# Six banks and a second gate buffer for the first feed-forward, and a later place for norm steps and projections

## The reference

```python
x = x + L0_attn(norm(x))   # 8 heads of 64, keys and values from a latent of 64
x = x + L0_ffn(norm(x))    # silu(x w1) * (x w2); gelu(. h1); gelu(. h2); . w3   (hidden 1024)
x = x + L1_attn(norm(x))   # 16 heads of 16, rotary positions on q and k
x = x + L1_ffn(norm(x))    # silu(x w_gate) * (x w_up); . w_down   (hidden 768)
```

## Time and profile before

| | |
|---|---|
| median of 3 runs | 2740.22 us (2734.58 to 2742.14) |
| the profiled execution | 2743.78 us, span 2741.9 us |
| PE busy | 2489.0 us, 91% of the span |
| DVE busy | 1502.1 us, 55% |
| ACT busy | 1357.9 us, 50% |
| POOL busy | 998.3 us, 36% |
| mean granted TensorE clock | 0.955 of full speed |

### The profile page before, as it was taken

The page is one execution under the profiler, slowest core; times in us unless marked ns, Lnnn a source line. Parts: engine busy times, 40 slices in busy tenths (PEclk is TensorE's granted clock), DMA queues, the critical chain, the costliest instruction groups (busy, mean ns, idle before and its releaser), DMA issues.

```text
span 2741.9 us, 38992 instructions
## 1 busy us (share of the span) xinstructions
PE 2489.0 (91%) x15333; PEld 1493.5 (54%) x15333; DVE 1502.1 (55%) x1965; ACT 1357.9 (50%) x1816; POOL 998.3 (36%) x656
## 2 busy tenths in 40 slices
PE   6888888888889799999999999999999999999888
PEld 4344444444444477777777777644444444443677
DVE  6555666566656322322122122378989889897454
ACT  3344444444334344444444444257777777778533
POOL 1454555555455534564564564420000000000333
PEclk8999999999999899999999999989999999999999
DMA  2111121211111243544544544523231312221222
GB/s 69 39 55 45 64 69 47 82 51 53 57 40 40 84 139 134 191 166 139 189 165 143 184 166 142 168 85 70 46 72 31 70 48 42 69 44 23 65 76 66
DMA packets 139912, 241.81 MB, mean 88 GB/s; under 512 B 28272, under 2 KB 88688, under 8 KB 139376
## 3 DMA queue, kind: packets, MB, share of 16 engines
q1 hardware_dynamic: 139728, 239.29, 28.5%
HBM read 198.20 MB, written 52.03 MB: 91 GB/s over the span
## 4 chain that ended last, share of the span: by engine, by line
PE 53%; DVE 3%; DMA 3%; ACT 3%; issue 2%; POOL 1%; SPq 1%; DVEq 0%; ACTq 0%; POOLq 0%
PE m_R L110 37%; PE m_O L110 10%; PE m_X L110 4%; DMA m_ln_x<-x 2%; DVE m_ln_x L181 1%; DMA x<-m_xres 1%; ACT m_P L1533 1%; PE m_X L202 1%; DVE m_ln_stat L159 1%; PE m_X L1930 1%; POOL m_ln_rstd L176 1%; SPq L1435 0%; ACT m_gate L1592 0%; POOL m_act0l L1814 0%; PE m_X L1938 0%
## 5 line engine op out<-in xcount | busy, mean ns | idle before, releaser
L1669 DVE TENSOR_REDUCE m_mraw<-m_R 128x2 f32<-128x1024 f32 x512 | 625.8, 1224 | 104.1 <-PE m_R L110 99.4
L1533 ACT ACTIVATE m_P<-m_R 128x1024 f32<-128x1024 f32 x512 | 524.4, 1026 | 170.3 <-PE m_R L110 167.7
L538 ACT ACTIVATE a_P<-a_S 128x1024 f32<-128x1024 f32 x256 | 248.6, 1023 | 178.2 <-PE a_S L110 178.2
L110 PE MATMUL m_O<-m_P,m_V 128*17 128x256 f32 x4096 | 333.6, 398 | 2.8 <-ACT m_P L1533 1.1
L110 PE MATMUL a_O<-a_P,a_V 128*64 128x512 f32 x1024 | 283.3, 680 | 0.0
L661 DVE TENSOR_REDUCE a_mraw<-a_X 128x2 f32<-128x1024 f32 x168 | 205.3, 1222 | 135.3 <-PE a_X L110 135.3
L1786 POOL TENSOR_TENSOR m_act0l<-m_xf,m_act0h 128x512 fp32r<-128x512 f32 x128 | 165.1, 1292 | 297.4 <-ACT m_xf L1597 167.3
L819 POOL TENSOR_TENSOR a_accp<-a_accp,a_P 128x1024 f32<-128x1024 f32 x96 | 229.1, 2386 | 87.5 <-ACT a_P L538 77.9
L110 PE MATMUL m_R<-m_Q,m_K 64*128 64x512 f32 x1024 | 259.1, 502 | 1.8 <-DVE m_mraw L1669 1.5
L110 PE MATMUL m_R<-m_act0l,m_wt 128*128 128x512 f32 x640 | 260.5, 407 | 0.0
L110 PE MATMUL m_R<-m_act0h,m_wt 128*128 128x512 f32 x640 | 259.8, 406 | 0.1
(11 more groups left out here) (231 smaller groups left out, 4302.1 us busy)
## 6 DMA issues: line engine op xcount, KB each, us to landing
m_wt<-wcopy SPq DMA_DIRECT2D x176, 512.0 KB, 3.3
m_ln_x<-x SPq DMA_DIRECT2D x24, 512.0 KB, 3.9
m_xres<-x SPq DMA_DIRECT2D x96, 128.0 KB, 3.2
m_K<-bounce_k SPq DMA_DIRECT2D x96, 128.0 KB, 4.2
m_Q<-bounce_q SPq DMA_DIRECT2D x192, 64.0 KB, 2.7
a_tile<-in_L_ffn_tiles SPq DMA_DIRECT2D x22, 512.0 KB, 3.7
wcopy<-in_L_ffn_tiles SPq DMA_DIRECT2D x22, 512.0 KB, 4.9
x<-m_xres SPq DMA_DIRECT2D x64, 128.0 KB, 2.1
```

The lines of the kernel that those rows point to most:

```text
L110: return pe.eng.matmul(out, lhsT, rhs, start=start, stop=stop, skip_group_check=True)
L538: act.eng.activation(P[n % NP][:, :, :], psS[n % 2][:, :, :], ACT.Exp, scale=SCALE).then_inc(s_exp)
L1533: act.eng.activation(P[h % 4][:, :, :], pair(key)[:, :, :], ACT.Exp, scale=SCALE).then_inc(R.free(key))
L1669: dve.eng.tensor_reduce(mraw[u % 2][:, at, :], pair(key)[:, :, :], AX.X, ALU.max).then_inc(R.free(key))
```

## The change

Ring Y gets six banks up to slot 480 and its two old ones after that. The gate has two buffers; the second is a part of the exponent buffer `P[3]`, for which the raw `wo` weights move to another tile (`TON`). ACT takes a gate tile of a slot before the high part of the up tile of the slot before. For the second attention, statistics, scaling, turns, projections and values move from slots 12 to 32 to slots 15 to 40; the next block's norm load, statistics and scaling move ahead, to slots 25, 32 and 36. The rope load moves from slot 42 to 46. In the last part, statistics and scaling go from slots 1 and 3 to 2 and 4. POOL's `norm.power` goes to the end of its slot.

```diff
-    C_LOAD, C_STATS, C_SCALE, C_TURN = 10, 12, 13, (14, 16)
-    PROJECT = {18: ("k", 0), 22: ("q", 0), 26: ("k", 1), 30: ("q", 1)}
-    VALUES = {20: 0, 24: 1, 28: 2, 32: 3}
-    B_LOAD, B_STATS, B_SCALE, B_TURN = 34, 40, 42, (46, 50)
+    C_LOAD, C_STATS, C_SCALE, C_TURN = 10, 15, 18, (22, 24)
+    PROJECT = {26: ("k", 0), 30: ("q", 0), 34: ("k", 1), 38: ("q", 1)}
+    VALUES = {28: 0, 32: 1, 36: 2, 40: 3}
+    B_LOAD, B_STATS, B_SCALE, B_TURN = 25, 32, 36, (46, 50)
@@ norm_at
-        if s in (1, 3) and k + 1 < NB:
-            return norm_of["d", k + 1], int(s == 3)
+        if s in (2, 4) and k + 1 < NB:
+            return norm_of["d", k + 1], int(s == 4)
@@
+    def y_slots():
+        early = sum(len(ended_at(H)) for H in range(START - ML - 8))
+        return [i % 6 if i < early else 4 + i % 2 for i in range(len(y_order()))]
@@
-        Y = Ring(p, "y", 2, y_order())
+        Y = Ring(p, "y", 6, y_order(), slots=y_slots())
@@
-        xf, gate = [...], p.sb("gate", [128, 512])
+        xf, gate = [...], [p.sb("gate", [128, 512])[:, :], P[3][:, 0, :]]
@@ sync
-                if s == 42 and 1 <= k < NB:
+                if s == 46 and 1 <= k < NB:
                     load_rope(k)
@@ leave (ACT; last_silu likewise)
-                    if g:
-                        act.wait_ge(*Y.emptied(("up", *divmod(g - 1, MT))))
+                    if g >= 2:
+                        act.wait_ge(*Y.emptied(("up", *divmod(g - 2, MT))))
@@ scalar loop
+                if send_high_at(H):
+                    send_high(*send_high_at(H)[1:])
+                for key in ended_at(H):
+                    if key[0] == "gate":
+                        leave(key)
                 for key in ended_at(H - 1):
                     if key[0] == "up":
                         gate_high(key)
@@ gpsimd loop
-                if norm_at(H) and norm_at(H)[1] == 0:
-                    norm.power(pool, norm_at(H)[0])
                 ...
                 if last_pair_at(H - 1):
                     last_low(*last_pair_at(H - 1))
+                if norm_at(H) and norm_at(H)[1] == 0:
+                    norm.power(pool, norm_at(H)[0])
```

More of the change, by code:

```diff
@@ L1232, in ffn_attention_ffn @@
         banks = p.ps("R", [128, 6, 512])
-        psO, psX, psY = p.ps("O", [128, 512]), [p.ps("X", [128, 512])], [banks[:, 4 + i, :] for i in range(2)]
+        psO, psX, psY = p.ps("O", [128, 512]), [p.ps("X", [128, 512])], [banks[:, i, :] for i in range(6)]
         psR = [[banks[:, 2 * i + j, :] for j in range(2)] for i in range(3)]
         X = Ring(p, "x", 1, x_order())
-        Y = Ring(p, "y", 2, y_order())
-        R = Ring(p, "pair", 3, pair_order(), slots=pair_slots(), before={2: [Y.emptied(key) for key in y_order()[-2:]]})
+        Y = Ring(p, "y", 6, y_order(), slots=y_slots())
+        last_y = {Y.slot(key): Y.emptied(key) for key in y_order()}
+        R = Ring(p, "pair", 3, pair_order(), slots=pair_slots(), before={i: [last_y[2 * i], last_y[2 * i + 1]] for i in range(3)})
         psD = [x for bank in psR for x in bank]
@@ L1260, in ffn_attention_ffn @@
         act_buf = [[p.sb(f"act{i}{j}", [128, MT, 512], F32R) for j in "hl"] for i in range(2)]
-        xf, gate = [p.sb(f"xf{i}", [128, 512]) for i in range(2)], p.sb("gate", [128, 512])
+        xf, gate = [p.sb(f"xf{i}", [128, 512]) for i in range(2)], [p.sb("gate", [128, 512])[:, :], P[3][:, 0, :]]
         yt = [p.sb(f"yt{i}", [128, 512]) for i in range(2)]
@@ L1589, in leave @@
                     g = 8 * key[1] + key[2]
-                    if g:
-                        act.wait_ge(*Y.emptied(("up", *divmod(g - 1, MT))))
-                    act.eng.activation(gate[:, :], bank[:, :], ACT.Silu, scale=scol[:, 0, key[2]:key[2] + 1]).then_inc(Y.free(key))
+                    if g >= 2:
+                        act.wait_ge(*Y.emptied(("up", *divmod(g - 2, MT))))
+                    act.eng.activation(gate[g % 2], bank[:, :], ACT.Silu, scale=scol[:, 0, key[2]:key[2] + 1]).then_inc(Y.free(key))
                 elif key[0] == "hidden":
@@ L1605, in last_silu @@
                 act.wait_ge(*Dr.filled(key))
-                if g:
-                    act.wait_ge(*Dr.emptied(("dup", *divmod(g - 1, LT))))
-                act.eng.activation(gate[:, :], psD[Dr.slot(key)], ACT.Silu, scale=SC).then_inc(Dr.free(key))
+                if g == 1:
+                    act.wait_ge(s_pv, NT * NU)
+                elif g >= 2:
+                    act.wait_ge(*Dr.emptied(("dup", *divmod(g - 2, LT))))
+                act.eng.activation(gate[g % 2], psD[Dr.slot(key)], ACT.Silu, scale=SC).then_inc(Dr.free(key))
             def last_high(k, m):
@@ L1725, in up @@
                 dve.wait_ge(s_lo, fs(key) - 1)
[L1726 removed]
+                dve.eng.scalar_tensor_tensor(xf[fs(key) % 2][:, :], psY[Y.slot(key)][:, :], scol[:, 1, key[2]:key[2] + 1], gate[g % 2],
                                              ALU.mult, ALU.mult).then_inc(Y.free(key))
@@ L1733, in last_up @@
                 dve.wait_ge(s_dlo, g - 1)
-                dve.eng.scalar_tensor_tensor(xf[g % 2][:, :], psD[Dr.slot(key)], SC, gate[:, :], ALU.mult, ALU.mult).then_inc(Dr.free(key))
+                dve.eng.scalar_tensor_tensor(xf[g % 2][:, :], psD[Dr.slot(key)], SC, gate[g % 2], ALU.mult, ALU.mult).then_inc(Dr.free(key))
             def last_residual(x):
```

9 lines of the change are left out of this document (4 added, 5 removed).

## The result

The changed kernel took 2662.1 us (median, 2652.3 to 2667.9), a ratio of 0.972 to the kernel before (95% interval 0.9685 to 0.976). Timed again beside two experiments it gave 2665.5 us against 2741.3, ratio 0.9725 (0.9711 to 0.9738), 75.9 us less. 2670 was forecast, 70 us less. The profiled execution took 2667.9 us, span 2666.1.

The account below looks back on a forecast made before the run. PE was taken to set the time, so only its waits and slow running could be won: 37.2 + 17.5 + 5.4 + 23.5 + 4 - 12.6 - 5 = 70 us off the 2740.2 median, 2670 us; range 2652 to 2692.

Parts of the forecast that it names:

- The wait in front of the turn: Feed-forward, blocks 1 to 7: PE's 37.2 us waiting for DVE's norm scaling goes, with 17.5 us of half clock.
- The cover of 1.7 us: Feed-forward turn moved eight slots later: at least 1.7 us of PE work left over, so the wait costs nothing.
- The eighth turn: Turn k = 8, in the second attention: its 3.94 us wait and 1.5 us of clock go, 5.4 us together.
- Six banks: Feed-forward gate and up products: small waits for a bank go, 2.9 us in each of eight blocks, 23.5 us.
- The new wait: Start of the second hidden layer: PE waits 2.1 us for POOL's low part in six blocks, 12.6 us back.
- The clock behind the new wait: Feed-forward: two of six blocks pay 2.5 us of slow clock after PE's wait for POOL, 5 us.
- The last part: After the second attention: shorter waits for the scaling, by 0.2 to 0.5 us in 7 blocks, and earlier out_low; 4 us.
- the sign given: Last part: 22.5 us a block would show the forecast right.
- (a): Feed-forward: POOL later than counted, clock falls each time; six waits cost 36 us instead of 17.6, 2688; chance 0.20.
- (b): Feed-forward: POOL in time because ACT or PE is later than counted; 17.6 us less, 2652; chance 0.13.
- (c): Feed-forward gates: small gaps are handovers that more banks don't remove; 23.5 us less gain, 2693; chance 0.11.
- (d): Weights come late behind the store's landing on SP, two tiles by 5 us each per block; 2754; chance 0.03.

Follow-up runs that it names:

- the second profile: The changed kernel unaltered, profiled again when timed beside two later kernels: 2665.5 us, ratio 0.9725 to the kernel before.
- The one-gate run: The changed kernel with one gate buffer and ScalarE's old order in the feed-forward, six banks kept: ratio 0.976 to the kernel before.
- later slots alone: The kernel before with only the last part's statistics and scaling one slot later and the power at the slot's end: ratio 0.9947.
- two buffers alone: The changed kernel with all slots and the power's place put back, keeping six banks, two gate buffers and ScalarE's new order: ratio 0.9894.
- the added product: The changed kernel with one more 1.25 us product in POOL's queue ahead of the rotation of k1: 2676.9 us, ratio 0.9791.
- a kernel without the wait: The changed kernel with later power, the low part inside the rotation of k1 and one gate buffer in the last part: 2641.5 us, ratio 0.964.
- the one-buffer kernels: Kernels with one gate buffer in the last part: the changed kernel so altered, ratio 0.9723; with later power and low part inside the rotation too, 0.964.
- the kernel with the later power: The changed kernel with the next block's statistics, scaling and power four slots later: 2653.9 us, ratio 0.9685.

## Why the prediction was right

The likeliest case came about. Its terms:

- **What bounds it.** Right: what was gained in the feed-forward is, but for 1.6 us, time in which PE stood or ran at half clock.
- **The wait in front of the turn, 37.2 us, and 17.5 for the clock.** Right, both gone; the ledger's 2.5 us of clock is the size that was forecast. The cover of 1.7 us held.
- **The eighth turn, 5.4 us.** Measured 4.9, from the transposes of the first unit's maxima in the second attention to those of the fifth's (116.3 us before, 111.4 after; 108.0 in the second profile). In all kernels with the early slots the whole second attention took 778.8 to 782.2 us, in all with the later ones 769.7 to 780.7.
- **Six banks, 2.9 us a block.** 2.6 (18.43 less 15.82). The one-gate run shows that banks, and not gate buffers, bring it; the second buffer is worth 0.4 us a block, which is the last up tile's low part that the prediction called a close fit.
- **The new wait, 2.1 us each, 12.6 in all.** 1.82, 10.9 in all, with its place and cause as named. Counted from the same P, POOL's low part ended at 22.7 (22.4 before the 0.4 for the scalings) and PE stood ready at 20.9 (20.7). The 0.4 us that I added for the scalings were wrong: under 0.1 came of them. I had read them from the earlier trace rows as POOL being put back; there POOL's two products beside the scalings took 1.26 us each, not longer than alone, and the 0.15 us between them was a wait for ScalarE. Block 7 has no power and no scalings in its queue, and its wait is 0.85, 0.97 less: the power. The wait for the query's DMA did go, as counted, but whole; of its 3.96 us only 0.85 came back. With these sizes the phase adds up to 37.2 + 17.5 + 20.9 + 3.1 - 10.9 - 4.7 = 63.1; 1.6 us of the 64.7 are not accounted for.
- **The rule of "SBUF — State Buffer", section "SBUF: two separate sides" of the Trainium skill**, by which POOL could stand for 1.4 us. The trace does not agree with that size: POOL's product beside the scalings took 1.35 us and not 1.29, while VectorE's four took 4.40 and not 1.38. In this queue VectorE stood, POOL hardly. What the last section shows of who starts first does agree with the rule.
- **The clock behind the new wait, 5 us.** 3 x 1.6 = 4.7 in one profile, 6 x 1.6 = 9.4 in the other. The size of one was too large and the number of blocks too small; how many there are changes from one execution to the next.
- **The last part, 4 us: the term that was mis-sized.** It brought 7.8 us (4.5 in the second profile), and little of it where the sum had it. The step had the scaling at +14.7 and it ends at +14.1. It took the scalings as slow as before, but only one whole product of POOL's, not two, now falls on them (2.57 us and not 3.43). The +14.7 does not follow from its own numbers either: 11.7 + 3.43 is 15.1. And the turns shown are the late ones. Over all seven, PE waits nearly as long as before, since two of them have gone from 0.89 to 1.86 us:

```profile
PE m_R L202 <- DVE m_ln_x L181: 18.6, 7, 3.7
```

```profile
PE m_R L202 <- DVE m_ln_x L181: 18.2, 7, 3.1
```

Before first, after second: 0.4 us. The other long waits of this part, for low parts of the norm and of the attention's output (the prediction mentions the latter without a price of their own), fell from 5.3 to 1.6 us. The rest is the clock, which was left out: the mean granted clock of the part went from 0.93 to 0.96, about 5 us, some of it inside the waits. In the second profile the turns wait 18.2 us again, the clock is 0.93 and the gain 4.5. A turn came every 21.5 us on average, where 22.5 was the sign given (22.8 before). The parts don't add: later slots alone bring 13.3 us by the profiles, two buffers alone 5.9. The prediction gave the two buffers no part in it, for or against.
- **The sum.** 75.9 us against 70; that the terms met so well is partly chance: in the first profile the feed-forward and the last part brought 4 us each more than forecast and the second attention 4 less, in the second profile the feed-forward brought 2 us less than forecast and the second attention 5 more.
- **Rivals.** (a) came about only with the added product (3.2 us a wait, five falls of six); its half about the clock also did in the second profile of the changed kernel, six of six behind 1.8 us. (b) did not: POOL was the last, and a kernel without the wait had to be built. (c) and (d) didn't occur.

## What to carry to other kernels

Write the engine's queue out instruction by instruction around the first consumer of a moved result: a microsecond put into a queue without a gap arrives whole at the engine that waits, and one taken out arrives until the queue begins to wait for something else. Where such a queue is full, putting the urgent instruction first only names another victim; look for the place between two dependent instructions of the long step where it costs its neighbours nothing. A second buffer lets work start earlier, and earlier can be just when it blocks something more urgent: ask of each buffer what will now run beside what.

## What was not expected of the hardware

- Beside GpSimd's products it was mostly VectorE's scalings that gave way. Four took 1.38 us alone, 1.61 and 2.57 with part of them beside a product, 4.37 to 4.40 against a full queue; the products of that queue lengthened from 1.29 us to at most 1.35. But which of the two had started first made the difference. A product that started behind a scaling already running was the one to get longer, by 0.1 us, and the scaling kept its 0.40: 1.38 and 1.39 us at the turns of the one-buffer kernels, 1.41 at 1196.57 in the kernel with the later power; behind two scalings it was 1.47 (at 1264.11 in the second profile of the changed kernel). In a queue without gaps a product is nearly always running when VectorE comes.
- The length of a wait did not decide by itself whether the clock fell. Behind the same 1.8 us it fell in three of six blocks in one execution and in six of six in another; behind 1.86 us at one turn of the last part it was 0.53, behind 2.92 at the next 1.00. Waits of 0.9 to 1.4 us in blocks 1 to 6 of the feed-forward were never followed by it. What decides between them stays open.
- The second attention, whose code is the same in all these kernels but for its first stretch, took between 769.7 and 780.7 us in the profiles of the kernels with the later slots. A difference of a few microseconds between two profiles has to be looked for in its own stretch.
